# Probabilities times V: two units at a visit in every second slot, in place of one in every slot

## What is computed

```python
# local: per window of 128 rows, over its own and the window before
attn = softmax(where(mask, -max, q @ k.T / 4))
out = attn @ v                  # b h n d, d = 16
h = h + out @ Wo + bo
# full: over all 512 rows of a batch
attn = softmax(q @ k.T / 4)
attn_out = attn @ v
h = h + attn_out + moe(layernorm(h))
```

## Time and profile before

| | |
|---|---|
| time, median of 3 runs | 600.5 us (600.39 to 601.75) |
| span of the profiled execution, first to last instruction | 600.7 us (no other time is given for it) |
| TensorE busy | 539.3 us, 90%, 3209 matmuls |
| VectorE busy | 424.7 us, 71% |
| ScalarE busy | 285.8 us, 48% |
| GpSimd busy | 188.1 us, 31% |
| times V (L1593) | 1024 matmuls, 107.2 us |
| row maxima of full stages (L1048) | 256, 170.8 us |

### The profile page before, as it was taken

One profiled execution on the slowest core, in us unless ns is written; L12 is line 12 of the kernel. 1 busy time (PEld: TensorE's weight loads), 2 busy tenths in 40 slices (PEclk: granted clock), 3 DMA queues, 4 the chain that ended last, 5 costly groups with the idle time before them and its releaser, 6 DMA issues.

```text
span 600.7 us, 9520 instructions
## 1 busy us (share of the span) xinstructions
PE 539.3 (90%) x3209; PEld 283.9 (47%) x3209; DVE 424.7 (71%) x941; ACT 285.8 (48%) x558; POOL 188.1 (31%) x257
## 2 busy tenths in 40 slices
PE   3968998989899899998888899989999999999996
PEld 2435554654565335334533456444545555544442
DVE  6757766667877895887678877656876566678841
ACT  0314454536544563676354343525565455444444
POOL 6444746223422600211243233202233331043201
PEclk9978999999999999999997899999999999999999
DMA  6364534222332343353235132403259667232311
GB/s 194 103 199 129 159 95 156 68 74 81 116 89 67 111 113 100 94 158 102 71 94 154 55 108 86 124 18 113 67 174 267 191 201 238 70 104 72 108 54 35
DMA packets 45151, 69.23 MB, mean 115 GB/s; under 512 B 9208, under 2 KB 38320, under 8 KB 42416
## 3 DMA queue, kind: packets, MB, share of 16 engines
q1 hardware_dynamic: 40672, 55.64, 31.5%
q0 software_dynamic: 4224, 12.59, 6.8%
q10 hardware_dynamic: 208, 0.40, 0.2%
HBM read 45.25 MB, written 23.07 MB: 114 GB/s over the span
## 4 chain that ended last, share of the span: by engine, by line
PE 67%; DVE 18%; issue 7%; DMA 3%; ACT 3%; POOL 1%; ACTq 0%; SPq 0%; DVEq 0%
PE OB L1593 12%; PE R L1473 10%; PE R L1368 9%; PE SC L1543 8%; PE ST L1566 7%; DVE neg_max L1048 5%; PE R L1383 4%; PE R L1459 4%; PE SC L1548 3%; PE ST L1572 2%; PE R L1419 2%; PE R L1487 2%; DVE neg_max L1056 2%; DMA QS<-shiftT 2%; PE SC L1553 2%
## 5 line engine op out<-in xcount | busy, mean ns | idle before, releaser
L1048 DVE TENSOR_REDUCE neg_max<-SC 128x1 f32<-128x512 f32 x256 | 170.8, 687 | 78.1 <-PE SC L1543 74.9
L909 ACT ACTIVATE prob<-ST 128x512 f32<-128x512 f32 x256 | 136.7, 598 | 123.9 <-PE ST L1566 118.7
L1593 PE MATMUL OB<-prob,VS 128*32 128x512 f32 (+2 forms) x1024 | 107.2, 491 | 0.1
L1543 PE MATMUL SC<-KS,QS 96*128 96x512 bf16 x256 | 97.6, 389 | 8.6 <-DVE neg_max L1048 6.6
L912 ACT ACTIVATE prob<-ST 128x512 f32<-128x512 f32 (+1 forms) x128 | 68.0, 543 | 68.2 <-PE ST L1572 67.9
L745 POOL TENSOR_SCALAR_AFFINE_SELECT prob<-prob 128x512 f32<-128x512 f32 x64 | 40.9, 639 | 131.1 <-ACT prob L912 131.0
L1566 PE MATMUL ST<-QS,KS 98*128 98x512 bf16 x256 | 77.5, 380 | 1.9 <-ACT prob L909 1.9
L1056 DVE TENSOR_REDUCE neg_max<-SC 128x2 f32<-128x512 f32 x64 | 44.1, 688 | 22.0 <-PE SC L1553 21.6
L1053 DVE TENSOR_REDUCE neg_max<-SC 128x1 f32<-128x128 f32 (+1 forms) x128 | 39.6, 351 | 25.8 <-PE SC L1553 25.5
L1548 PE MATMUL SC<-KS,QS 96*128 96x256 bf16 (+1 forms) x256 | 48.0, 270 | 6.2 <-DVE neg_max L1053 2.7
L1543 PEld LDWEIGHTS SC<-KS,QS 96*128 96x128 bf16 x256 | 24.8, 97 | 55.1 <-DVE neg_max L1048 35.9
(11 more groups left out here) (156 smaller groups left out, 765.1 us busy)
## 6 DMA issues: line engine op xcount, KB each, us to landing
scratch<-parts SPq DMA_DIRECT2D x96, 128.0 KB
QS<-scratch SPq DMA_DIRECT2D x42, 256.0 KB, 3.3
KS<-scratch SPq DMA_DIRECT2D x42, 256.0 KB, 3.9
x_sorted<-ys SPq DMA_DIRECT2D x24, 128.0 KB, 3.2
xs<-x_sorted SPq DMA_DIRECT2D x12, 256.0 KB
y_sorted<-ys SPq DMA_DIRECT2D x12, 256.0 KB
QS<-scratch SPq DMA_DIRECT2D x12, 128.0 KB, 2.6
w_exp<-in_L_ffn_W_experts SPq DMA_DIRECT2D x6, 256.0 KB, 3.3
```

The source lines that it names most:

```text
L909: act.activation(prob[:, u % 2, e, :], src[:, :], ACT.Exp, scale=SCALE).then_inc(s_prob, 1)
L1048: dve.tensor_reduce(own_max[:, i, head:head + 1], bank[:, :], AX.X, ALU.max, negate=True).then_inc(s_max, 1)
L1543: pe.matmul(bank[:, :], Q[0:SHIFT_ROW, head, i * P:(i + 1) * P], K[0:SHIFT_ROW, head, :], start=True, stop=True).then_inc(s_sc_ps, 1)
L1593: mm = pe.matmul(OB[VW * i:VW * (i + 1), columns], VS[s % 3][:, kt, v:v + VW], p_of, start=(kt == 0), stop=(kt == NT - 1), skip_group_chec ...
```

## The change

In full stages, where two units are multiplied in a slot, they stand in the slot's first half, behind three of the unit's four scores; unit `u - 2` and then `u - 1`, in even slots. In local stages the pair is units `u - 3` and `u - 2`, in odd slots, where the single one stood. A stage's last two units are multiplied in the next stage's first slot. In the last stage slots 11 to 15 and the end keep one unit at a time, in the place of before. ScalarE's copy of a group's output follows the same list; no product, copy or DMA is added or left out.

```diff
-PV_LAG = (2, 1)
+PV_LAG = (3, 2)
+ALONE_FROM = 10
...
 def units_times_v(s, u):
-    units = []
-    if u == 0 and s > 0:
-        units.append((s - 1, UNITS - 1))
-    if PV_LAG[STAGES[s][0]] <= u < UNITS:
-        units.append((s, u - PV_LAG[STAGES[s][0]]))
-    return units
+    if u == 0:
+        return [(s - 1, UNITS - 2), (s - 1, UNITS - 1)] if s > 0 else []
+    if s == LAST and u > ALONE_FROM:
+        return [(s, u - 1)]
+    first = u - PV_LAG[STAGES[s][0]]
+    return [(s, first), (s, first + 1)] if first >= 0 and first % 2 == 0 else []
...
                 per = BANKS[kind] // 2
+                units = units_times_v(s, u)
                 for e in range(per):
                     scores(s, u, e)
                 for step in quarters[0]:
                     row_scores(*step)
+                early = kind == FULL and len(units) == 2
+                if early:
+                    scores(s, u, per)
+                    for step in units:
+                        times_v(*step)
                 half_slot(s, 2 * u, quarters[1])
-                for e in range(per, 2 * per):
+                for e in range(per + early, 2 * per):
                     scores(s, u, e)
                 for step in quarters[2]:
                     row_scores(*step)
-                for step in units_times_v(s, u):
-                    times_v(*step)
+                if not early:
+                    for step in units:
+                        times_v(*step)
                 half_slot(s, 2 * u + 1, quarters[3])
-                if kind == LOCAL and u == UNITS - 1:
-                    times_v(s, u - 1)
```

## The result

The changed kernel takes 607.1 us (median of 5 runs, 605.6 to 607.5) against 600.4 for the kernel before on the same chip (5 runs, 599.1 to 601.8): a ratio of 1.0103, 95% interval 1.0075 to 1.0132. It is slower by 6.7 us, and above the range that was forecast. The profiled execution has a span of 605.8 us; its own time was 607.5, so some 1.7 us lie outside the first and last instruction. In the code after, the lines behind 200 have one number more: V is L1594, the experts' sums are L1211, the maxima L1049. In most of the kernels edited further, lines are another five on (V is L1599).

A forecast was written before the change was run, and what follows sets the result against it. TensorE was taken to bound the full stages. Saved 6.0 + 7.2, given back 4.8 + 4.2 + 1.9, a gain of 2.3 us from a median of 600.5: 598.2 us, within a range of 591.5 to 604.5.

The forecast's parts named there:

- part 3: Full-stage slots losing their V visit: TensorE's waits for VectorE to free banks, hidden by V before, cost 4.8 us.
- part 5: Stage-end shifts leave later and the next group's scores wait, 1.9 us lost; ScalarE's later exponentials in even slots cost nothing.
- the sign of being wrong that was named last: ScalarE's exponentials coming to end waits of the scores would show the prediction wrong; no size given.
- part 1: All stages: 61 fewer visits to V, each costing 0.20 us besides its products; saves 2.8 full, 3.2 local, sum 6.0.
- VectorE sets the odd slots: Full stages' odd slots: VectorE's work exceeds what TensorE has left, so removed visits return as waits; 603.0 to 606.2, chance 0.25.
- The Trainium skill's rule: Weight loads overlap running matmuls only where row groups differ; second units would wait for weights, 603.3 us, chance 0.06.
- Part 2: Full stages' even slots and the last stage's third rows: the pair covers TensorE's waits there, saving 7.2 us.
- Part 4: Full stages: rows come before the maximum two rows earlier is done; 6.3 us if each stood alone, two thirds taken, 4.2 lost.

The follow-up runs named there:

- the runs with one half each: Changed kernel with units paired in the full stages alone, 606.5 us; or in the local stages alone, 601.0 us.
- the place alone: Kernel before, nothing paired; in full stages the one unit moves behind the third scores: 605.2 us, 1.0088 of before.
- the first combined version: Kernel before with pairs in stage 2 only and, in the last stage's slots 1 to 14, one unit behind three scores: 594.8 us, 0.9899.

## Why the prediction was wrong

It forecast 598.2 us with a gain, and the change loses 6.7. Three steps failed: part 3, whose list of new waits in the full stages was too short by 3.1 us; part 5, which put ScalarE at nothing, where the scores wait 2.2 us for it (the sign of being wrong that was named last); and part 1's 3.2 us in the local stages, which didn't come. The rival that came nearest is that VectorE sets the odd slots (603.0 to 606.2), though its point, the odd slot's missing visit, is only a part of it. By the steps:

- **Part 1, fewer visits.** In the full stages right and a little low: 0.23 a pair for 0.20. The Trainium skill's rule (TensorE: Matmul & The Clock Gate, Part 3), by which the second unit's loads would stand in the open, doesn't hold between units either: the second unit costs 0.86 us. In the local stages the step failed: 3.2 were expected for visits on the chain of waits, and the measured effect is nothing (0.9 us of loss, between 1.1 of gain and 3.1 of loss). At the end of stage 0 the shift's DMA, which TensorE already waited for, took that stage's gain; stage 4 was longer, with the clock low for longer. How much each took of the rest is not shown.
- **Part 2, waits that the pair covers.** Of the four waits at a slot's first job three vanished, and the third rows' waits in the last stage's even slots too; in stage 6 TensorE's waits for VectorE's normalising went from some 4.4 us (start to start) to nothing, where 2.7 were booked. The fourth, 0.48 at 499.52, stayed, at 0.40. The profile named no releaser for it, and the step took it to vanish like the others; it ends with a readout that itself waits for the DMA of the expert outputs. That readout before, and after with the wait of TensorE:

```profile
498.77 0.69 DVE L1196 COPY ys<-R 128x512 f32<-128x512 f32 x1 [1.45 <-DMA y_sorted<-ys]
```

```profile
505.99 0.69 DVE L1197 COPY ys<-R 128x512 f32<-128x512 f32 x1 [2.85 <-DMA y_sorted<-ys]
...
506.73 1.13 PE L1460 MATMUL R<-w_k,xsT 128*128 128x256 f32 x4 [0.40 <-DVE ys L1197]
```

VectorE's waits for this DMA (us in all, times, longest), before and after:

```profile
DVE ys L1196 <- DMA y_sorted<-ys: 2.6, 2, 1.4
```

```profile
DVE ys L1197 <- DMA y_sorted<-ys: 5.5, 2, 2.8
```

That stage 6 is only 0.1 us shorter all the same is parts 3 and 4: its waits for readouts (`ys`) grew by 2.7 us and those for maxima by 2.5.

- **Part 3, waits that V hid.** The slots named there came as worked out: 1.09 more in slots 9 and 10 of stage 5, 0.83 for 0.8 in slot 8, 0.71 for 0.7 in slot 5 of stage 3, 0.88 for 1.09 in slot 14 of stage 6. The list was too short: slots 3, 7, 13 and 15 of stage 5 wait 2.1 us together for the sums, and slots 3, 7 and 11 of stage 6 another 1.1 for readouts. The step counted only slots where TensorE waited already, and not those where V's visit covered the wait whole.
- **Part 4, the rows' two banks.** Counted from start to start, waits for maxima and late first rows grew by about 4 us in the full stages, against 4.2 in the sum.
- **Part 5.** The shift at the end of stage 3 is right: TensorE waits 1.4 us longer for its DMA, against 1.3. ScalarE, costed at nothing, was not: in stages 3 and 5 the fourth scores wait 2.2 us for exponentials that had to wait for the pair.

By halves, against the runs with one half each: the sum makes the full stages 0.9 us slower (2.8 + 7.2 - 4.8 - 4.2 - 1.9), and they were 6.3 slower; it makes the local stages 3.2 faster, and they were 0.9 slower. For the 5.4 by which the full stages are off there are the missing slots of part 3 (3.1), part 5's exponentials (2.2) and part 2's fourth wait (0.6). These terms don't simply add, as a late slot gives the next wait room, and an estimated 2 us of the loss go with the clock (last section), which the sum doesn't have. Against the 2.3 us of gain that were forecast, the missing slots alone, or the local gain alone, turn the sign. That part 4's count came out at 4 is in part luck, as the two thirds in it were a guess.

## What to carry to other kernels

A block of work on the bounding engine, standing between what another engine consumes and what it must give back, is that engine's time to catch up; before moving it, follow the other engine's queue from the block's start to its end and write down every release that falls into it, also those that show no wait now. A wait that a move covers is worth only the distance to the next thing that is late, here a DMA that the trace shows as a wait on another engine. And try a change's parts stage by stage: here the place alone gained 4.4 us in one stage and lost 9 in three others.

## What the runs showed that was not expected

The time is less steady than the few first runs told: 25 runs of the kernel before, in one group, lie between 596.0 and 603.5 us. In the profiles TensorE's granted clock is 0.50 (the 1.2 GHz level, against 2.4) in stretches that lie above all ahead of stage 0 and in stage 4, where of all stages TensorE waits most: in stage 4 it was 10.3 us in two stretches before, and in the profile of the first combined version, whose median is 594.8, 27.3 without a break:

```profile
311.20:338.50 27.30, 25.52 (x127) 9.11 (x128) 19.51 (x43) 7.35 (x15) 4.78 (x10) 0.50 0.30 89
```

That stage took 65.4 us in that profile and 60.7 before, with the same order in it. Whether the change itself lengthens such stretches stays open: in all five profiles with pairs in stage 0 the clock fell at the start of stage 1, behind the wait for the shift, but it did so in three of eight without them as well.

The clock has a share in the loss. Each run has a mean granted clock: its median is 0.980 in those 25 runs and 0.976 in the five of the changed kernel. With levels of 0.50 and 1.00 alone, that is some 24 and 29 us at the lower. Over the 62 runs of the kernel before that stand beside the experiments (two far ones, 605.9 and 646.4 us, left out) a run is 0.31 us longer for each us more at the lower level, with a correlation of 0.85. From this an estimated 2 us of the 6.7 go with the clock, and some 4.5 stay at a like clock. Whether it is the waits opened by the change that bring the clock down, no run here tells.
